# Small scalar steps of two norms moved from VectorE to GpSimd, and the input x moved to another DMA queue

## The reference

```python
x = x + tanh(g_xattn[0]) * xattn_0(_layernorm(x), ctx)   # queries and keys from ctx, softmax, mixes x's features
x = x + tanh(g_ffn[0])   * ffn_0(_layernorm(x))          # two quantised linear layers (bit_linear)
x = x + tanh(g_xattn[1]) * xattn_1(_layernorm(x), ctx)   # 16 heads, queries and keys RMS-normed
x = x + tanh(g_ffn[1])   * ffn_1(_layernorm(x))          # router, 8 of 64 experts, a shared expert

def bit_linear(x, w, g):                                 # ffn_0: gate/up (256 to 2 x 704), then down (704 to 256)
    xn = x * rsqrt(mean(x * x) + EPS) * g
    scale = 127.0 / clip(max(abs(xn)), 1e-5, None)       # per token
    xq = clip(round(xn * scale), -128, 127) / scale
    wq = clip(round(w / c), -1, 1) * c                   # c = clip(mean(abs(w)), 1e-5, None)
    return xq @ wq.T
```

## Time and profile before

| | us |
|---|---|
| median of 3 runs (lowest to highest) | 672.39 (672.16 to 672.51) |
| profiled execution, its own time | 672.21 |
| span of that execution | 670.4 |
| TensorE busy | 620.6 |
| VectorE busy | 496.1 |
| ScalarE busy | 426.2 |
| GpSimd busy | 226.9 |

### The profile page before, as it was taken

One profiled execution on the slowest core, in us unless ns is written; L12 is line 12 of the kernel. 1 busy time (PEld: TensorE's weight loads), 2 busy tenths in 40 slices (PEclk: granted clock), 3 DMA queues, 4 the chain that ended last, 5 costly groups with the idle time before them and its releaser, 6 DMA issues.

```text
span 670.4 us, 11775 instructions
## 1 busy us (share of the span) xinstructions
PE 620.6 (93%) x3658; PEld 531.0 (79%) x3658; DVE 496.1 (74%) x1179; ACT 426.2 (64%) x1086; POOL 226.9 (34%) x223
## 2 busy tenths in 40 slices
PE   5656577999999999999999999999999999999997
PEld 3534366899999999999998887887888788888886
DVE  3779985776677877867887677877777677777776
ACT  3675756898888888878888744454444444444442
POOL 4532838575556655656667301000000000000000
PEclk9876989999999999999999999999999999999999
DMA  8200010211200000000004044443654335545540
GB/s 311 90 2 23 0 50 23 95 49 46 75 1 1 2 1 2 1 1 1 1 2 118 2 140 142 153 134 118 187 159 156 115 118 185 160 156 156 156 133 32
DMA packets 24724, 55.35 MB, mean 83 GB/s; under 512 B 4064, under 2 KB 4704, under 8 KB 24544
## 3 DMA queue, kind: packets, MB, share of 16 engines
q1 hardware_dynamic: 24384, 53.66, 25.5%
q10 hardware_dynamic: 288, 1.05, 0.4%
HBM read 53.39 MB, written 1.31 MB: 82 GB/s over the span
## 4 chain that ended last, share of the span: by engine, by line
PE 77%; ACT 4%; DVE 4%; issue 3%; POOL 1%; DVEq 0%; ACTq 0%; POOLq 0%
PE bank L268 22%; PE bank L270 22%; PE bank L269 22%; PE bank L695 4%; PE bank L675 2%; PE bank L667 2%; PE bank L730 1%; ACT att L1190 1%; PE bank L627 1%; PE bank L620 1%; POOL u L421 1%; PE bank L545 0%; ACT front_hi L1406 0%; DVE shift L1673 0%; DVE attT_lo L1678 0%
## 5 line engine op out<-in xcount | busy, mean ns | idle before, releaser
L1223 ACT ACTIVATE inter_hi<-inter 128x512 fp32r<-128x512 f32 x63 | 39.8, 632 | 143.3 <-DVE inter L1779 141.5
L270 PE MATMUL bank<-xnT_hi,front_lo 128*128 128x512 f32 (+1 forms) x260 | 102.6, 395 | 0.0
L268 PE MATMUL bank<-xnT_hi,front_hi 128*128 128x512 f32 (+1 forms) x260 | 102.2, 393 | 0.0
L269 PE MATMUL bank<-xnT_lo,front_hi 128*128 128x512 f32 (+1 forms) x260 | 101.7, 391 | 0.0
L1783 DVE TENSOR_TENSOR inter_lo<-inter,inter_hi 128x512 fp32r<-128x512 f32 x63 | 43.6, 693 | 45.7 <-ACT inter_hi L1223 45.7
L1190 ACT ACTIVATE att<-bank,shift,rq 128x256 f32<-128x256 f32 x128 | 71.2, 570 | 0.6 <-DVE shift L1673 0.6
L448 POOL TENSOR_TENSOR att<-att,rowinv 128x512 f32<-128x512 f32 x64 | 66.7, 1062 | 10.0 <-DVE rowinv L1683 9.9
L432 POOL TENSOR_TENSOR rk<-msq,minus_half 128x4 f32<-128x4 f32 x32 | 32.2, 1007 | 106.7 <-DVE msq L1655 94.1
L1666 DVE TENSOR_REDUCE rowmax<-bank 128x2 f32<-128x512 f32 x64 | 43.8, 685 | 27.6 <-PE bank L270 26.3
L1752 DVE TENSOR_TENSOR prod<-gate_s,bank 128x512 f32<-128x512 f32 x63 | 43.2, 686 | 21.3 <-PE bank L270 19.5
L269 PEld LDWEIGHTS bank<-xnT_lo,front_hi 128*128 128x128 f32 x260 | 48.8, 188 | 11.4
(11 more groups left out here) (261 smaller groups left out, 1841.7 us busy)
## 6 DMA issues: line engine op xcount, KB each, us to landing
w_all<-w_rows SPq DMA_DIRECT2D x128, 128.0 KB, 2.9
raw<-in_expert_w SPq DMA_DIRECT2D x32, 384.0 KB, 3.5
wvo_raw<-in_expert_w SPq DMA_DIRECT2D x16, 384.0 KB, 3.5
e_more<-in_expert_w SPq DMA_DIRECT2D x16, 384.0 KB, 3.6
wvo_raw<-in_head_vo SPq DMA_DIRECT2D x8, 384.0 KB, 3.3
raw<-in_head_qk SPq DMA_DIRECT2D x8, 384.0 KB, 3.2
gate_raw<-in_gate_wT SPq DMA_DIRECT2D x1, 1408.0 KB, 8.9
x<-in_x_tok ACTq DMA_DIRECT2D x2, 512.0 KB, 6.5
```

Of the source, the lines that this page charges most:

```text
L268: pe.matmul(out, l_hi, r_hi_, start=start, stop=False, skip_group_check=True)
L269: pe.matmul(out, l_hi, r_lo_, start=False, stop=False, skip_group_check=True)
L270: return pe.matmul(out, l_lo, r_hi_, start=False, stop=stop, skip_group_check=True)
L1223: act.activation(inter_hi[:, slot, :], inter[:, slot, :], ACT.Copy).then_inc(a_Ihi, 1)
```

## The change

Five parts.
1. Small steps ahead of a root go from VectorE to GpSimd: the add of EPS in `stats_0`, `stats_2` and `stats_1`, and the mean square of `mean_h`, which is gone. GpSimd now does the step and then the power, with a wait for itself between (`link_g`). It also negates the means (`negm`) for its own normalisation.
2. The clamp of the largest value at EPS is folded into the gains: g1 and g2 are multiplied by GAIN = 127 / EPS once, on GpSimd (`scale_gain`), and the scale to quantise with is the smaller of 127 / absmax and the root: one reciprocal and one step on VectorE. The scales to go back by are made on GpSimd (`scale_back_1`, `scale_back_2`), and `silu_0` and `add_down` wait for them.
3. The order on GpSimd: `normalise_1(0)` stands ahead of `times_gain(3)`, and `root_2(1)` and `root_2(2)` one gain product earlier; the new steps are put between.
4. x is loaded on SP's queue, behind the context, the weights, the bias and the gains.
5. The energies of the first two batches stand ahead of the last product of `query_key`.

```diff
+GAIN = 127.0 / EPS
...
+            for h in range(2):
+                sp.dma_start(x[:, 4 * h:4 * h + 4, :], x_tok[:, 4 * h:4 * h + 4, :]).then_inc(l_x[h], 16)
             sp.dma_start(gate_raw[:, :, :], gate_wT).then_inc(l_gate, 16)
...
             def root_0(b):
                 c = slice(2 * b, 2 * b + 2)
-                power(v_pw1, b, vare[:, c], rstd[:, c], 2, g_pw1)
+                pool.wait_ge(v_pw1, b + 1)
+                pool.tensor_scalar(negm[:, c], mv[:, c, 0], -1.0, 0.0, ALU.mult, ALU.add)
+                link_g(pool, pool.tensor_scalar(vare[:, c], mv[:, c, 1], 1.0, EPS, ALU.mult, ALU.add))
+                pool.tensor_tensor(rstd[:, c], vare[:, c], minus_half[:, 0:2], ALU.pow).then_inc(g_pw1, 1)
...
             def root_2(b):
                 c = slice(2 * b, 2 * b + 2)
-                power(v_pw3, b, tinyB[:, 5, c], tinyB[:, 6, c], 2, g_pw3)
+                pool.wait_ge(a_h1, 2 * b + 2)
+                link_g(pool, pool.tensor_scalar(tinyB[:, 5, c], sumh[:, c], 1.0 / INTER, EPS, ALU.mult, ALU.add))
+                pool.tensor_tensor(tinyB[:, 6, c], tinyB[:, 5, c], minus_half[:, 0:2], ALU.pow).then_inc(g_pw3, 1)
...
+            def scale_gain(gain, loaded):
+                pool.wait_ge(loaded, 16)
+                pool.tensor_scalar(gain[:, :], gain[:, :], GAIN, 0.0, ALU.mult, ALU.add).then_inc(g_gain, 1)
+
+            def scale_back_1(b):
+
+                c = slice(2 * b, 2 * b + 2)
+                pool.wait_ge(v_sc1, b + 1)
+                if b == 0:
+                    pool.wait_ge(v_abs, 1)
+                    pool.tensor_scalar(wsk[:, 0:1], wsc[:, 0:1], 1.0 / (127.0 * GAIN), 0.0, ALU.mult, ALU.add)
+                link_g(pool, pool.tensor_tensor(tinyB[:, 8, c], tinyB[:, 3, c], tinyB[:, 1, c], ALU.mult))
+                pool.tensor_scalar(tinyB[:, 4, c], tinyB[:, 8, c], 127.0, wsk[:, 0:1], ALU.max,
+                                   ALU.mult).then_inc(g_sc1, 1)
...
-                    pool.tensor_scalar(u[:, i, :], x[:, i, :], mv[:, i, 0:1], rstd[:, i:i + 1], ALU.subtract,
+                    pool.tensor_scalar(u[:, i, :], x[:, i, :], negm[:, i:i + 1], rstd[:, i:i + 1], ALU.add,
                                        ALU.mult).then_inc(g_u0, 1)
...
+            scale_gain(g1, l_g1)
             root_1(0)
+            scale_gain(g2, l_g2)
+            scale_back_1(0)
             pool.wait_ge(a_ctx, 2)
...
             root_2(0)
+            scale_back_1(1)
             root_1(3)
+            scale_back_2(0)
+            scale_back_1(2)
+            scale_back_1(3)
             rms_k(0)
             times_gain(2)
             root_3(0)
+            normalise_1(0)
             times_gain(3)
-            normalise_1(0)
             times_gain(4)
+            root_2(1)
             times_gain(5)
-            root_2(1)
             times_gain(6)
+            root_2(2)
+            scale_back_2(1)
             times_gain(7)
-            root_2(2)
             rms_q(0)
             root_2(3)
+            scale_back_2(2)
             normalise_att(0, 0)
             normalise_att(0, 1)
+            scale_back_2(3)
             rms_k(1)
...
             query_key(0, 1, 4)
-            query_key(1, 1, 7)
             pe.wait_ge(a_qkA, 2)
             energy(0, 5)
             energy(1, 6)
+            query_key(1, 1, 7)
             pe.wait_ge(a_qkA, 4)
...
-            act.dma_start(x[:, 0:4, :], x_tok[:, 0:4, :]).then_inc(l_x[0], 16)
-            act.dma_start(x[:, 4:8, :], x_tok[:, 4:8, :]).then_inc(l_x[1], 16)
...
                 act.wait_ge(t_y1, i + 1)
+                act.wait_ge(g_sc1, i // 2 + 1)
...
             def stats_0(b):
-                tile_stats(2 * b, 2 * b + 2)
-                ask_rstd(2 * b, 2 * b + 2, v_pw1)
+                tile_stats(2 * b, 2 * b + 2).then_inc(v_pw1, 1)
...
                 link(dve, dve.tensor_reduce(T[:, 3, c], w1[:, c, :], AX.X, ALU.max, apply_absolute_value=True))
+                link(dve, dve.reciprocal(T[:, 10, c], T[:, 3, c]))
...
                 dve.wait_ge(g_pw2, b + 1)
-                link(dve, dve.tensor_tensor(T[:, 5, c], T[:, 3, c], T[:, 1, c], ALU.mult))
-                link(dve, dve.tensor_scalar(T[:, 6, c], T[:, 5, c], EPS, None, ALU.max))
-                link(dve, dve.reciprocal(T[:, 7, c], T[:, 6, c]))
-                dve.tensor_scalar(T[:, 4, c], T[:, 6, c], 1.0 / 127.0, wsc[:, 0:1], ALU.mult, ALU.mult)
-                link(dve, dve.scalar_tensor_tensor(T[:, 3, c], T[:, 7, c], 127.0, T[:, 1, c], ALU.mult, ALU.mult))
+                dve.scalar_tensor_tensor(T[:, 2, c], T[:, 10, c], 127.0, T[:, 1, c], ALU.mult,
+                                         ALU.min).then_inc(v_sc1, 1)
+                dve.wait_ge(v_sc1, b + 1)
...
                 dve.wait_ge(v_amax, 2 * b + 2)
+                link(dve, dve.reciprocal(T[:, 11, c], amax2[:, c]))
                 dve.wait_ge(g_pw3, b + 1)
-                link(dve, dve.tensor_tensor(T[:, 2, c], T[:, 6, c], amax2[:, c], ALU.mult))
-                link(dve, dve.tensor_scalar(T[:, 3, c], T[:, 2, c], EPS, None, ALU.max))
-                link(dve, dve.reciprocal(T[:, 7, c], T[:, 3, c]))
-                dve.tensor_scalar(T[:, 5, c], T[:, 3, c], 1.0 / 127.0, wsc[:, 1:2], ALU.mult, ALU.mult)
-                link(dve, dve.scalar_tensor_tensor(T[:, 2, c], T[:, 7, c], 127.0, T[:, 6, c], ALU.mult, ALU.mult))
-                link(dve, dve.tensor_scalar(T[:, 7, c], T[:, 5, c], tg[:, 2:3], None, ALU.mult))
+                dve.scalar_tensor_tensor(sc2[:, c], T[:, 11, c], 127.0, T[:, 6, c], ALU.mult,
+                                         ALU.min).then_inc(v_sc2, 1)
+                dve.wait_ge(v_sc2, b + 1)
...
                 dve.wait_ge(t_y2, i + 1)
+                dve.wait_ge(g_sc2, i // 2 + 1)
...
-            dve.wait_ge(l_g1, 16)
+            dve.wait_ge(g_gain, 1)
             times_g1(0)
```

More of the change, by code:

```diff
@@ L140, in link, with link_g @@
             dve.wait_ge(v_link, link_n[0])
-        v_pw1, v_pw2, v_pw3, v_pw4, v_pw5 = (sem(f"v_pw{i}") for i in range(1, 6))
+        g_link = sem("g_link")
+        g_link_n = [0]
+        def link_g(pool, ins):
+            g_link_n[0] += 1
+            ins.then_inc(g_link, 1)
+            pool.wait_ge(g_link, g_link_n[0])
+        v_pw1, v_pw2, v_pw4, v_pw5 = (sem(f"v_pw{i}") for i in (1, 2, 4, 5))
         g_pw1, g_pw2, g_pw3, g_pw4, g_pw5 = (sem(f"g_pw{i}") for i in range(1, 6))
+        g_gain, v_sc1, v_sc2, g_sc1, g_sc2 = (sem(n) for n in ("g_gain", "v_sc1", "v_sc2", "g_sc1", "g_sc2"))
         g_u0, t_u0, a_x0 = sem("g_u0"), sem("t_u0"), sem("a_x0")
@@ L402, in root_2 @@
+                link_g(pool, pool.tensor_scalar(tinyB[:, 0, c], mv[:, c, 1], 1.0 + EPS, EPS * EPS, ALU.mult, ALU.add))
+                pool.tensor_tensor(tinyB[:, 1, c], tinyB[:, 0, c], minus_half[:, 0:2], ALU.pow).then_inc(g_pw2, 1)
             def root_2(b):
                 c = slice(2 * b, 2 * b + 2)
-                power(v_pw3, b, tinyB[:, 5, c], tinyB[:, 6, c], 2, g_pw3)
+                pool.wait_ge(a_h1, 2 * b + 2)
+                link_g(pool, pool.tensor_scalar(tinyB[:, 5, c], sumh[:, c], 1.0 / INTER, EPS, ALU.mult, ALU.add))
@@ L406, in root_3 @@
+                pool.tensor_tensor(tinyB[:, 6, c], tinyB[:, 5, c], minus_half[:, 0:2], ALU.pow).then_inc(g_pw3, 1)
             def root_3(b):
                 c = slice(2 * b, 2 * b + 2)
-                power(v_pw4, b, vare[:, c], rstd[:, c], 2, g_pw4)
+                pool.wait_ge(v_pw4, b + 1)
+                pool.tensor_scalar(negm[:, c], mv[:, c, 0], -1.0, 0.0, ALU.mult, ALU.add)
+                link_g(pool, pool.tensor_scalar(vare[:, c], mv[:, c, 1], 1.0, EPS, ALU.mult, ALU.add))
+                pool.tensor_tensor(rstd[:, c], vare[:, c], minus_half[:, 0:2], ALU.pow).then_inc(g_pw4, 1)
@@ new lines, in scale_back_2 @@
+            def scale_back_2(b):
+                c = slice(2 * b, 2 * b + 2)
+                pool.wait_ge(v_sc2, b + 1)
+                if b == 0:
+                    pool.wait_ge(v_abs, 2)
+                    pool.wait_ge(a_tg, 1)
+                    pool.tensor_scalar(wsk[:, 1:2], wsc[:, 1:2], 1.0 / (127.0 * GAIN), tg[:, 2:3], ALU.mult, ALU.mult)
+                link_g(pool, pool.tensor_tensor(tinyB[:, 9, c], amax2[:, c], tinyB[:, 6, c], ALU.mult))
+                pool.tensor_scalar(tinyB[:, 7, c], tinyB[:, 9, c], 127.0, wsk[:, 1:2], ALU.max,
+                                   ALU.mult).then_inc(g_sc2, 1)
@@ L466, in _ @@
             root_1(2)
-            pool.wait_ge(l_g2, 16)
+            pool.wait_ge(g_gain, 2)
             times_gain(0)
@@ L1530, in stats_1 @@
             def stats_1(b):
-                c = slice(2 * b, 2 * b + 2)
                 dve.wait_ge(v_xA, b + 1)
-                tile_stats(2 * b, 2 * b + 2)
-                dve.tensor_scalar(T[:, 0, c], mv[:, c, 1], 1.0 + EPS, EPS * EPS, ALU.mult,
-                                  ALU.add).then_inc(v_pw2, 1)
+                tile_stats(2 * b, 2 * b + 2).then_inc(v_pw2, 1)
+                dve.wait_ge(v_pw2, b + 1)
```

(4 more changed lines are left out.)

31 lines of the change are left out of this document (13 added, 18 removed).

## The result

The changed kernel takes **652.54 us** in the median of 4 runs (651.18 to 654.77), beside 672.27 of the kernel before in 4 runs (668.01 to 672.51): a ratio of 0.9724, interval 0.9676 to 0.9773. 19.7 is the difference of the two medians; the ratio, taken of the means, makes 18.6 of it, since one of the four executions of the kernel before took only 668.01 us. The profiled execution of the changed kernel took 654.77 us (span 653.0), the longest of the four, so the spans show only 17.4.

A forecast was written before the change was run, and what follows sets the result against it. Before 115 us no engine was held full, so the last transposed rows of stage B set the gain; behind that TensorE is nearly full. Terms 2.8 + 0.7 + 2.2 + 2.0 + 0.65 = 8.35 gave 664.0 us, range 661.0 to 669.0.

The forecast's parts named there:

- four normalisations 4.86, ... two normalisations 2.87: At the start, GpSimd's normalisations around its second root would last 4.86 and 2.87 us, ending at 23.0 instead of 26.76.
- normalise_1(0) 2.46: Between 57 and 84 us, GpSimd's normalisation moved ahead of times_gain(3) was taken to last 2.46 us.
- the first term: At the start, x behind the context lets products begin at 4.9 and weight_scale(0) come at 27.1 instead of 29.89: 2.8 us.
- The small steps: Two-column multiplies or adds on GpSimd: 0.25 us each with hand-over, ends 0.10 and 0.71; twelve on the path.
- the second to the fourth term: Fewer VectorE steps: 0.7 us in scales_1(0), 2.2 in the second block (50 to 56 us), 2.0 from 57 to 84.
- The fifth: From 84 to 115 us: TensorE's 0.90 wait for low_w(2) goes, root_3(3) costs 0.25; gain 0.65 us.
- VectorE stands at times_g1(0) until 24.3: At the start, VectorE would wait at the gain product until GpSimd has scaled g1, at 24.3 us.
- Scaling the gains: GpSimd's scaling of g1 was priced at 1.2 us and of g2 at 3.3; g2's was let block nothing.
- the clock falls less: Rival, 84 to 115 us: shorter waits bring back half of TensorE's lost clock, 1.7 us, giving 662.3; chance 0.12.
- The order on GpSimd: 57 to 84 us: absmax_2(3), behind the delayed times_gain(3), stands and eats what its own stalls give back.
- Slower: GpSimd becomes the bound: Rival: on twelve path places, small steps of 0.99 us use up the gain; at 1.2 the time is 675; chance 0.03.
- The context does not come earlier: Rival at the start: both queues share full engines, so the 2.8 us gain goes, giving 666.8; chance 0.10.

The follow-up runs named there:

- e2: The changed kernel with GpSimd's normalisations subtracting the mean again, all else kept: 663.93 us, ratio 0.9902 to the kernel before.
- e12: The kernel before with the negated mean added, x on SP's queue and two energies ahead of the last product; small steps, clamp and order unchanged: 659.42 us.
- e8: The changed kernel with only the normalisations' add made a subtract, the negated mean still the operand (results wrong by twice the mean): 662.33 us.
- e11: The changed kernel with TensorE's idle time filled by unread transposes, and the normalisations subtracting the mean again: 661.19 us.
- e5: The changed kernel with normalise_1(0), root_2(1) and root_2(2) back at their old places on GpSimd: 651.72 us.
- e10: The changed kernel with TensorE's idle time filled by unread transposes, and GpSimd's order of before: 648.86 us.
- e1: The kernel before with one change: GpSimd negates the means and normalises by adding them instead of subtracting the mean: 662.71 us.
- e7: The changed kernel with 34 and 12 unread transposes filling TensorE's idle time in two places: 649.46 us.

## Why the prediction was wrong in size, step by step

The gain of each stretch, from the start times in the profiles (the first times_up_0 stands at the end of the second, the second block's turned rows, 56.33 before and 43.89 after, at the end of the third). Of VectorE in the kernel before, the first times_up_0 and the last turned rows:

```profile
46.89 0.95 DVE L1585 SCALAR_TENSOR_TENSOR hs<-bank,tinyB,hs 128x704 f32<-128x704 f32 x1 [3.05 <-PE bank L602]
...
116.13 0.69 DVE L1506 TENSOR_TENSOR xnT_lo<-bank,xnT_hi 128x512 fp32r<-128x512 f32 x1 [1.89 <-ACT xnT_hi L1097]
```

| up to | forecast | after | e2 | after against e12 |
|---|---|---|---|---|
| weight_scale(0) | 2.8 | 6.57 | 2.92 | 0.21 |
| first times_up_0 | 0.7 | 3.58 | 3.58 | 0.73 |
| second block turned | 2.2 | 2.29 | 2.28 | 2.30 |
| first scores | 2.0 | 2.37 | 1.46 | 2.05 |
| last turned rows | 0.65 | 1.99 | -1.06 | -0.84 |
| sum | 8.35 | 16.80 | 9.18 | 4.45 |

- **The step that failed** is "four normalisations 4.86, ... two normalisations 2.87", and later "normalise_1(0) 2.46". These durations were taken over from the rows of before, although the diff changes the instruction itself: the mean is no longer subtracted but its negative added, and a tile costs 0.57 to 0.58 us instead of 1.25. Six tiles behind the third block's root save 6 x 0.67 = 4.0 us; the first term was missed by 3.77, and with the subtraction (e2) it is 2.92, the forecast's 2.8. The last norm is the second place: from the scores to the last rows e2 takes 33.15 us, after 30.10. All sixteen tiles save 16 x 0.67 = 10.7 us of GpSimd's time, and e2, e8 and e11 show 9.8 to 11.7 us of the whole; alone on the kernel before it is 7.5. The prediction read the negation as a small step that is added, and never asked what it was there for.
- **The small steps were right.** 0.19 us each, 0.25 to 0.28 with the hand-over (13.25 to 13.50 to 13.78), forecast 0.25. Some took longer beside VectorE's work, 0.3 to 0.5 us, and one 1.62 (see the last section). The gain of the second block is 2.29 (2.2). Against e12, which has the fast normalisation but none of the small steps, the second to the fourth term are 0.73, 2.30 and 2.05, as forecast (0.7, 2.2, 2.0). The fifth, 0.65, is not confirmed: -0.84, in profiles whose clock differs there (0.72 against 0.86 from 75 to 85 us).
- **The start was right in its mechanism.** Products 4.94 (4.9), first maximum 10.66 (10.35). "VectorE stands at times_g1(0) until 24.3" did not happen; weight_scale(0) waits in VectorE's own queue, which is full from 18.89 us on. It did happen in e2, where a tile costs what the forecast took: the wait ended at 24.40 and weight_scale(0) came at 26.97 (27.1). In part that is luck, since errors of the sum cancel there: the third block's root began at 13.83 instead of 12.9, for GpSimd was still normalising; the last pair took 2.44, not 2.87; and scaling g1 took 0.41, not 1.2.
- **Scaling the gains** was priced at 1.2 and 3.3 us by the normalisation's row; it took 0.41 and 0.77. That row was again one with the subtraction, and with operands of its own for each partition where the scaling has constants. The difference of the two lengths is 0.36 us for 448 columns, 0.8 ns per column. With the small step's 0.191 us as the fixed part, an estimate, the add with two per-partition operands costs (0.573 - 0.191) / 256 = 1.5 ns and the subtraction (1.246 - 0.191) / 256 = 4.1 ns. The Trainium skill, page "GPSIMD Engine Reference", section "3.1 Elementwise — side-by-side cycle accounting", states about 1.8 cycles per element at 1.2 GHz, 1.5 ns, as the best case of GpSimd's loop; the add agrees with it, the subtraction doesn't.
- **The clock.** The rival "the clock falls less" got 0.12 and a price of 1.7 us between 84 and 115. The clock did fall less, but at 41 to 46 us, where it gave 2.84, and a new low stretch came at 70 to 81. The second term's excess is this, and it is the same in e2, whose sum comes near the forecast only because this gain and the -1.06 at the end offset each other: e2 confirms the terms up to the second block, not the whole sum.
- **The order on GpSimd** was held to cost (VectorE's fourth absmax_2, `absmax_2(3)`, standing behind `times_gain(3)`). The wait is there, 1.37 us ahead of 61.24, and with the order of before it is 0.17 in e5 and 0.19 in e10; but the kernel is then at most about 1 us faster, within the spread.
- **"Slower: GpSimd becomes the bound"** asked for small steps of 0.99 us with their hand-over; they are a quarter of that. "The context does not come earlier" is refuted by the products at 4.94.

The remainder is 8.45 us of stretches that gained more than forecast, 3.77 + 2.88 + 0.09 + 0.37 + 1.34, and the medians have 2.2 us more, as the profiled execution of after was by so much the longer one.

## What to carry to other kernels

A duration read from a trace holds for one operation with one set of operands; where the diff alters the instruction, even one ALU operation in it, that row is no longer its price, and a part that looks like preparation (a negated mean) is a sign of it. On GpSimd, a tensor_scalar of a 128 x 256 fp32 tile with two per-partition operands took less than half the time with an add in place of the subtract, and negating the two columns of its operand cost 0.19 us. If TensorE idles ahead of dense work, compare the spacing of its matmuls at both levels before the gain or loss is put down to the edit: here idle time filled with transposes nobody reads gave 3 us.

## What the runs showed of the hardware

- GpSimd's tensor_scalar on 128 x 256 fp32 with two per-partition operands: subtract and multiply 1.23 to 1.28 us, add and multiply 0.55 to 0.59 us, in the means of eight tiles each of before, e2 and e8, and of after and e1. The subtract costs this with the mean and with the negated mean as its operand (e2, e8).
- GpSimd and VectorE hold each other up in both directions. Two pairs in the timeline of after:

```profile
25.62 1.63 DVE L1630 TENSOR_SCALAR gate_raw<-gate_raw 128x2816 f32<-128x2816 f32 x1
25.67 1.62 POOL L445 TENSOR_SCALAR wsk<-wsc 128x1 f32<-128x1 f32 x1 [2.73 <-DVE tinyB L1609]
```
```profile
68.81 1.70 POOL L478 TENSOR_TENSOR w<-hs,g 128x704 f32<-128x704 f32 x1
...
69.05 1.48 DVE L1709 TENSOR_SCALAR msq<-ssq 128x4 f32<-128x4 f32 x1
```

  One column on GpSimd took 1.62 us, until VectorE's clip beside it was done (27.25); four columns on VectorE took 1.48, until GpSimd's gain product was done (70.51). The rule weighed in the prediction (the Trainium skill, page "SBUF — State Buffer", section "SBUF: two separate sides") agrees with both. Its counter-example in the prediction stands all the same: in the kernel before, two tensor_scalars of VectorE (25.48) took 0.76 us, against 0.62 for the same two at 35.06, inside one of GpSimd's normalisations, which took 1.32 us where the median of its line is 1.23. Neither waited there for the other's end; why a gain product held VectorE up and a normalisation did not stays open. The case for which it was weighed, the scaling of g2 ahead of the clip, did not arise: g2 was done at 22.93, the clip began at 25.62. The step on GpSimd that was held up is one the change adds; the scales it makes are wanted only later.
- TensorE's granted level turned inside one product: the scores' matmuls went from 0.12 to 0.21 us apart at 70.4 us, behind waits of 0.72 and 1.82 us, and came back at 80.6. In e7, where transposes fill part of those waits, the same matmuls stayed 0.12 apart.
